# Attention with paged keys: products with new values on 32 rows, in pairs in the banks of the scores, added to the outputs by VectorE

## The chip, the cores and the metric

The kernel runs on one core of one Trainium2 chip. The metric is the device time of one execution in microseconds (us). Durations of single instructions come from one profiled execution.

## The reference

Two blocks with residuals over x (64 sequences, 32 positions, 512 channels). Block 0 is a state-space convolution over the positions and a feed-forward layer with low-rank experts. Block 1 is attention with a paged cache of keys and values, and another such feed-forward layer. The change lies in block 1's attention:

```
q, k, v = x Wq, x Wk, x Wv          # 32 query heads, 8 key heads, head size 128
q, k = rope(rmsnorm(q)), rope(rmsnorm(k))
k_all = [cache pages of the sequence (512 keys), its own 32 new keys]
v_all = [cache pages of the sequence (512 values), its own 32 new values]
probs = softmax(q k_all / sqrt(128), cached keys beyond the length masked out)
o = probs v_all                      # 4 query heads share one key head
out = o Wo
```

## The kernel before

The program has a prologue, block 0's feed-forward layer, the projection of queries, keys and values, attention, the output projection and block 1's feed-forward layer. A tensor `ps` covers PSUM: 8 banks of 128 partitions by 512 floats.

**Units, groups, batches.** `attention()` (from L1075) works through 512 units. A unit is one key head of one sequence (called a batch here): its four query heads times 32 positions make 128 rows of scores over 544 keys. Four units make a group (QU = 4), eight a batch (UB = 8), 16 one turn of the written-out loop (PER). There are 128 groups and 64 batches.

**Steps.** `turns` (L711) writes the loop of each engine as steps. In step u an engine does the stage "live(d)" for unit u - d; j is u within its turn plus the lead. So a unit passes through the engines over some ten steps:

- SP loads, per batch: the queries (L1122), 16 pages of keys (L1133, their numbers are read from the page table by L1129), the new keys (L1136), and the new values (L1141, `load_v`); then `store` sends the reciprocals of the sums (L1147) and the outputs `ot` of the batch (L1149). These are one queue in program order: for batch b it holds queries b+2, keys b+2, new values b+2, store b. The store waits for `s_o`, which ScalarE's copy of `ot` increments.
- VectorE splits the keys of two heads into an upper part in step u - 2 for even heads (`k_hi`, L1303) and a rest for odd heads (`k_lo`, L1306). PE's scores of an even head wait for the rest (`s_lo`). The first split of a batch, in steps 8b+2, waits for its keys. In steps 8b+2 and 8b+6 it also splits the queries' rest (`q_lo`, L1351), in steps 8b+3 it makes the mask (L1325).
- PE, u - 4: three products of the scores on split operands (L1227), into banks 0 and 1 for even units and 2 and 3 for odd ones; the 544 columns lie in the middle, columns 256 to 799 of each two banks. `wait(e, s_max, m - 1)` keeps it off banks that VectorE has not reduced.
- VectorE, u - 4: scales, masks, takes the row's extreme (L1319), to SBUF. ScalarE: exponential with row sums (L1392).
- PE, u - 6: four transposes of the probabilities of cached keys (L1236). ScalarE copies them to SBUF (L1379). Once a group, in step u - 7, one transpose takes the group's probabilities of new keys, 4 x 32 columns, to 128 rows (L1247), and ScalarE copies them to `pt_new` (L1384).
- PE, u - 8: products of the cached values with the transposed probabilities (L1260), summed in bank 5 or 6, one bank a group, 128 columns a unit.
- PE, u - 9, once a group: four products with new values (L1267). `v_new` holds the 32 new values of head k in rows 32k to 32k+31 and zeros elsewhere, so that a whole 128-row product gives head k's part only, and it goes onto the same sums:

```
for k in range(QU):
    last = e.matmul(sums(w, k), v_new[q][:, g // QU, k * D:(k + 1) * D], pt_new[:, w, :],
                    start=False, stop=(k == QU - 1), skip_group_check=True)
last.then_inc(s_nw, 1)
```

- ScalarE, u - 10, once a group: copies the bank to `ot` (L1374), increments `s_o`.
- POOL gathers the cached values of batch b+2 (L1182) once PE's new products of batch b are done (`s_nw`).

A float32 product is two records of PE in the trace, each with its weight load; a float32 transpose is one.

The last turn's steps are written out. There VectorE also does work for the output projection: L1333, L1339 and, in step PER+6, the split L1343 of the first outputs. The projection's first product (L1552) waits for `s_max`, its second unit for ScalarE's last copy.

In the prologue, L398 multiplies operands of 64 rows (upper and lower half in turn, 32 columns), between whole-array transposes of L386.

Of the kernel before, what the change touches and what calls it, by code (L numbers as in the profile page):

```python
# [19 lines left out]
ALU = mybir.AluOpType  # L20
# [3 lines left out]
P = 128  # L24
B, S, L = 64, 32, 512
# [12 lines left out]
KC = LK // P  # L38
# [658 lines left out]
def wait(eng, sem, value):  # L697

    if not isinstance(value, int) or value > 0:
        eng.wait_ge(sem, value)  # L700
# [374 lines left out]
def attention(nc, block, sems, ps, dram, cst, k_t, qk_t, v_own, o_t, ri_d, keys, results, early, projected, late):  # L1075
# [12 lines left out]
    with ExitStack() as ctx:  # L1088
# [12 lines left out]
        pt_new = sb("pt_new", [P, 2, P])  # L1101
        rt = sb("rt", [UB, 2, P])
        s_rows = sem("rows")
        s_v, s_one, s_idx, s_mask, s_qlo, s_hi, s_lo, s_s, s_max, s_e, s_ri, s_nc, s_c, s_cn, s_pt, s_wn, s_rt, s_nw, s_o = (
            sem(n) for n in ("v", "one", "idx", "mask", "qlo", "hi", "lo", "s", "max", "e", "ri", "nc", "c", "cn",
                             "pt", "wn", "rt", "nw", "o"))
        s_passed = [sem("passed_pool"), sem("passed_vector")]
        s_vr, s_vn = ([sem(f"{n}{q}") for q in range(2)] for n in ("vr", "vn"))
# [4 lines left out]
        turned = lambda w: ps[:, 6 - w, 0:2 * P]  # L1113
        sums = lambda w, k: ps[:, 5 + w, k * P:(k + 1) * P]

        steps = lambda e, step: turns(e, B * UB, PER, 12, step)

        @block.sync
        def _(e):
# [24 lines left out]
            def store(b, q):  # L1144
                e.wait_ge(s_rt, b + 1)
                at = bass.ds(b, 1) if not isinstance(b, int) else slice(b, b + 1)
                e.dma_start(ri_d[:, at, :].rearrange("g o x -> g (o x)"), rt[:, q, :]).then_inc(s_ot[q], 16)  # L1147
                e.wait_ge(s_o, (b + 1) * 2 + 1)
                e.dma_start(o_t[at, :, :].rearrange("o d x -> (o d) x"), ot[:, q, :]).then_inc(s_ot[q], 16)  # L1149

            e.wait_ge(s_in, 32)
            e.wait_ge(*own_stored)
            for q in range(2):
                e.wait_ge(s_one, q + 1)
                load_v(q, q)
            with e.Fori(0, B // 2 - 1) as i:
                for q in range(2):
# [20 lines left out]
        @block.gpsimd  # L1178
        def _(e):
            def gather_values(q):  # L1180
                for c in range(KC):
                    e.indirect_dma_start(out=v_raw[:, q, c, :], out_offset=None, in_=dram["v_cache"],  # L1182
                                         in_offset=bass.IndirectOffsetOnAxis(ap=idx[:, q, c:c + 1], axis=0)).then_inc(s_vr[q], 16)

            def indices(b, q):

                cols = slice(b * KC, (b + 1) * KC) if isinstance(b, int) else bass.ds(b * KC, KC)
                e.tensor_copy(idx[:, q, :], rows[:, cols]).then_inc(s_idx, 1)  # L1188

            e.wait_ge(s_qr, NQU * NT)  # L1190
            e.wait_ge(s_rows, 1)
            for q in range(2):
                indices(q, q)
                e.wait_ge(s_idx, q + 1)
                gather_values(q)
            e.wait_ge(s_proj, tiles - NT)
            e.memset(v_new[0][:, :, :], 0.0).then_inc(s_one, 1)
            e.wait_ge(s_proj, tiles)
            e.memset(v_new[1][:, :, :], 0.0).then_inc(s_one, 1)
            with e.Fori(0, B // 2 - 1) as i:  # L1200
                for q in range(2):
                    b = i * 2 + q
                    wait_apart(e, s_passed[0], (s_nw, (b + 1) * 2))
                    indices(b + 2, q)
                    wait_apart(e, s_passed[0], (s_idx, b + 3))
                    gather_values(q)

        @block.tensor
        def _(e):
            ident = cst[:, C_ID:C_ID + P]  # L1210

            def step(i, j, u, live):
                if live(4):
                    m, jj = u - 4, j - 4
                    g, q, r, w = jj % UB, (jj // UB) % 2, jj % 2, (jj // 2) % 2
                    if isinstance(u, int) and u < 6:
                        e.wait_ge(s_stage, tiles - 2 + 2 * (u - 4))
                    if g % QU == 0:
                        e.wait_ge(s_qlo, i * 4 + jj // QU + 1)
                    if g % 2 == 0:  # L1220
                        e.wait_ge(s_lo, i * UB + jj // 2 + 1)
                    wait(e, s_max, m - 1)
                    mine = slice(g * P, (g + 1) * P)
                    upper, lower = q_hi[:, q, mine], q_lo[q][:, mine]
                    for a, b, first, end in ((upper, k_hi, True, False), (upper, k_lo, False, False), (lower, k_hi, False, True)):
                        for part in (slice(0, W), slice(W, NKEY)):
                            last = e.matmul(scores(r)[:, part], a, b[:, w, g % 2, part],  # L1227
                                            start=first, stop=end)
                    last.then_inc(s_s, 1)
# [18 lines left out]
                if live(8):  # L1248
# [9 lines left out]
                    e.wait_ge(s_pt, m + 1)  # L1258
                    for c in range(KC):
                        e.matmul(sums(w, k), v_raw[:, q, c, g * D:(g + 1) * D], pt[:, jj % 4, c * P:(c + 1) * P],  # L1260
                                 start=(k == 0 and c == 0), stop=False, skip_group_check=True)
                if live(9) and (j - 9) % QU == QU - 1:
                    jj = j - 9
                    g, q, w = jj % UB, (jj // UB) % 2, (jj // QU) % 2
                    e.wait_ge(s_wn, i * 4 + jj // QU + 1)
                    for k in range(QU):
                        last = e.matmul(sums(w, k), v_new[q][:, g // QU, k * D:(k + 1) * D], pt_new[:, w, :],  # L1267
                                        start=False, stop=(k == QU - 1), skip_group_check=True)
                    last.then_inc(s_nw, 1)

            steps(e, step)

        @block.vector
        def _(e):
# [9 lines left out]
            v(lambda e: e.tensor_copy(lenf[:, :], leni[:, :]))  # L1284
            e.memset(mask[:, :, LK:NKEY], 0.0)
            e.wait_ge(s_qt, NQU * NT)

            def step(i, j, u, live):
                if live(6) and (j - 6) % QU == QU - 1:
# [20 lines left out]
                    split(j - 2)  # L1310
                if isinstance(u, int) and u == 4:
                    split(3)
                if live(4):
                    m, jj = u - 4, j - 4
                    q, r, k, w = (jj // UB) % 2, jj % 2, jj % QU, (jj // QU) % 2
                    at = slice(w * QU + k, w * QU + k + 1)

                    wait_apart(e, s_passed[1], (s_mask, i * 2 + jj // UB + 1), (s_s, m + 1), (s_e, m - 1))
                    e.tensor_tensor_reduce(out=sm[:, r, :], in0=scores(r), in1=mask[:, q, :],  # L1319
                                           scale=-SC, scalar=3e38, op0=ALU.add, op1=ALU.min,  # L1320
                                           accum_out=nm[:, at]).then_inc(s_max, 1)
# [40 lines left out]
        def _(e):  # L1362
# [47 lines left out]
                    e.activation(q_hi[:, q, :], qk[:, q, :], ACT.Copy).then_inc(s_qhi, 1)  # L1410

            steps(e, step)
        return s_max, s_nw, s_o


def by_head(x):
# [11 lines left out]
def output_projection(nc, block, sems, ps, dram, o_t, ri_d, results, late, attended):  # L1428
# [7 lines left out]
    PER = 2 * CB  # L1436
    sem = lambda n: sems.enter_context(nc.semaphore("op_" + n))
    w_raw, o_raw, ri_b, s_w, s_o, s_on, s_ot = results
    s_max, s_nw, s_copied = attended
    att, inputs = late.att, late.inputs  # L1440
    w_hi, w_lo, o_hi, o_lo = late.w_hi, late.w_lo, late.o_hi, late.o_lo
    s_whi, s_wlo, s_ohi, s_olo = late.s_whi, late.s_wlo, late.s_ohi, late.s_olo
# [31 lines left out]
    def _(e):  # L1474
# [6 lines left out]
                e.tensor_tensor(w_lo[par][:, r, :], w_raw[:, r, :], w_hi[par][:, r, :].bitcast(F32),  # L1481
                                ALU.subtract).then_inc(s_wlo, 1)
        e.wait_ge(s_nw, 2 * B)
        e.wait_ge(s_copied, 2 * B + 1)
        inputs.clear(e)
        halve(1, 1)
        with e.Fori(1, HK // 2) as i:
# [48 lines left out]
    def _(e):  # L1536
        def step(i, j, u, live):
# [4 lines left out]
                e.wait_ge(s_wlo, (i * 2 + j // CB + 1) * REP)  # L1542
            if isinstance(u, int) and u == 0:
                e.wait_ge(s_max, B * HK)
            if isinstance(u, int) and u == 1:
                e.wait_ge(s_copied, 2 * B + 1)
            e.wait_ge(s_ohi, u + 1)
            wait(e, s_acc, (u - 1) * KB)
            for ob in range(KB):
# [123 lines left out]
```

## Time and profile before

| | |
|---|---|
| Median of 3 runs | 2424.05 us (2423.72 to 2424.26) |
| Profiled execution | 2424.02 us, its span 2421.9 us |
| PE busy (matmuls) | 2374.0 us, 98% of the span |
| PE's weight loads | 2159.3 us, 89% |
| VectorE (DVE) | 1873.6 us, 77% |
| ScalarE (ACT) | 1320.2 us, 55% |
| GpSimd (POOL) | 720.4 us, 30% |
| Moved by DMA | 542.35 MB, 224 GB/s |

Busy time of PE counts the pipelined end of each matmul, so it says that PE never paused, not that it was used fully. The distance of starts in the timeline is what an instruction costs a stream. "x4" counts merged instructions, "[0.68 <-PE ...]" is the idle time of the engine before the row and what ended it. PEld is the weight load of PE, SPq the DMA queue of SP. Attention lies between some 790 and 1993 us.

### The profile page before, as it was taken

What the parts mean: (1) busy time and instruction counts of PE and PEld (TensorE: products, weight loads), DVE (VectorE), ACT (ScalarE), POOL (GpSimd) and SP (SyncE); (2) the same over time, 40 slices, a digit from 0 to 9 for tenths busy, and PEclk for the clock granted to TensorE, in tenths of its full rate; (3) what the DMA queues carried; (4) which work ended last, traced back from release to release, by engine and by line L of the source; (5) the groups of instructions that cost most, each with busy time, mean ns of one, the idle gap of its engine ahead of it and who ended that gap; (6) DMA issues with size and microseconds to landing.
All of it is one profiled execution on the core that took longest, in us unless ns stands there. A gap on an engine that the chain in (4) does not pass through costs nothing. (4 is left out here: it accounts for less than half of the span.)

```text
span 2421.9 us, 53973 instructions
## 1 busy us (share of the span) xinstructions
PE 2374.0 (98%) x16104; PEld 2159.3 (89%) x16104; DVE 1873.6 (77%) x3303; ACT 1320.2 (55%) x3759; POOL 720.4 (30%) x713
## 2 busy tenths in 40 slices
PE   5999999999999999999999999999999999999999
PEld 4888787887778999999999999999999998888877
DVE  6559999999961787888888888888888876666653
ACT  3335555555543777777777777777777771111120
POOL 2006666666641122222222222222222213131100
PEclk8999999999999999999999999999999999999999
DMA  9633333333337787888888888888888879665622
GB/s 340 237 122 92 95 95 95 97 116 95 96 119 238 241 302 278 294 302 297 289 285 297 301 294 282 292 300 304 285 285 298 301 268 295 217 224 198 219 70 104
DMA packets 434116, 542.35 MB, mean 224 GB/s; under 512 B 36980, under 2 KB 350100, under 8 KB 429460
## 3 DMA queue, kind: packets, MB, share of 16 engines
q1 hardware_dynamic: 391300, 398.43, 48.2%
q0 software_dynamic: 36864, 134.23, 16.4%
q10 hardware_dynamic: 5904, 9.06, 1.1%
q8 instruction: 28, 0.46, 0.1%
q14 instruction: 20, 0.16, 0.0%
HBM read 440.59 MB, written 101.01 MB: 224 GB/s over the span
## 5 line engine op out<-in xcount | busy, mean ns | idle before, releaser
L1319 DVE CUSTOM_DVE_ANT_0 at_sm<-ps,at_mask 128x544 f32<-128x544 f32 x512 | 370.1, 723 | 232.0 <-PE ps L1227 225.5
L1260 PE MATMUL ps<-at_pt,at_v_raw 128*128 128x128 f32 x4096 | 540.8, 275 | 0.0
L1260 PEld LDWEIGHTS ps<-at_pt,at_v_raw 128*128 128x128 f32 x4096 | 497.6, 192 | 0.0
L1379 ACT ACTIVATE at_pt<-ps 128x512 f32<-128x512 f32 x512 | 305.9, 598 | 292.2 <-PE ps L1236 279.7
L954 POOL TENSOR_TENSOR pr_m<-pr_qn,tb 128x256 f32<-128x256 f32 x320 | 331.3, 1054 | 311.4 <-DVE pr_qn L923 296.2
L1392 ACT ACTIVATE at_pr<-at_sm,at_nm 128x544 f32<-128x544 f32 x512 | 383.7, 750 | 15.6 <-DVE at_nm L1319 11.5
L1306 DVE TENSOR_TENSOR at_k_lo<-shared,at_k_hi 128x1088 fp32r<-128x1088 f32 x256 | 325.9, 1273 | 0.0
L772 PE MATMUL ps<-pr_hi,xh 128*128 (+1 forms) x768 | 317.5, 413 | 5.9 <-DVE pr_qn L923 4.8
L1182 POOL DMA_INDIRECT at_v_raw<-v_cache,at_idx x256 | 277.8, 1085 | 113.5 <-issue 62.1
L1236 PE MATMUL ps<-constants,at_pr 128*128 128x128 f32 x2048 | 306.9, 272 | 0.1
L774 PE MATMUL ps<-pr_hi,xl 128*128 (+1 forms) x768 | 303.2, 395 | 0.0
L773 PE MATMUL ps<-pr_lo,xh 128*128 (+1 forms) x768 | 303.0, 394 | 0.0
L880 ACT ACTIVATE pr_sq<-ps 128x128 f32<-128x128 f32 x640 | 168.6, 278 | 227.6 <-DVE f_a L916 222.2
L1188 POOL COPY at_idx<-at_rows 128x4 uint32 (+1 forms) x64 | 12.0, 188 | 852.3 <-PE ps L1267 786.2
L1227 PE MATMUL ps<-at_k_hi,at_q_hi 128*128 128x256 f32 (+1 forms) x1024 | 254.1, 329 | 0.6 <-issue 0.6
L1236 PEld LDWEIGHTS ps<-constants,at_pr 128*128 128x128 f32 x2048 | 243.1, 141 | 0.3 <-ACT at_pr L1392 0.3
L1227 PE MATMUL ps<-at_k_hi,at_q_lo 128*128 128x256 f32 (+1 forms) x1024 | 212.1, 289 | 0.0
L1227 PE MATMUL ps<-at_k_lo,at_q_hi 128*128 128x256 f32 (+1 forms) x1024 | 211.1, 287 | 0.0
L1500 ACT ACTIVATE op_ohi<-o_raw 128x2048 fp32r<-128x2048 f32 x31 | 59.5, 1920 | 268.2 <-PE ps L1557 223.7
L1552 PE MATMUL ps<-op_ohi,op_whi 128*128 128x512 f32 x512 | 199.3, 389 | 0.0
L1553 PE MATMUL ps<-op_ohi,op_wlo 128*128 128x512 f32 x512 | 199.2, 389 | 0.0
L934 DVE TENSOR_TENSOR pr_m<-pr_qn,ta 128x512 f32<-128x512 f32 x160 | 195.8, 1224 | 0.0
(233 smaller groups left out, 4283.6 us busy)
## 6 DMA issues: line engine op xcount, KB each, us to landing
shared<-k_t SPq DMA_DIRECT2D x1024, 128.0 KB, 4.1
qk_t<-pr_stage SPq DMA_DIRECT2D x160, 256.0 KB, 2.2
shared<-qk_t SPq DMA_DIRECT2D x64, 512.0 KB, 7.9
o_t<-at_ot SPq DMA_DIRECT2D x64, 512.0 KB
shared<-ri_d SPq DMA_DIRECT2D x32, 1024.0 KB, 8.3
o_raw<-o_t SPq DMA_DIRECT2D x32, 1024.0 KB, 6.0
f_w<-wqkv SPq DMA_DIRECT2D x12, 1024.0 KB, 6.1
s_k_in<-k_cache SPq DMA_DIRECT2D x16, 512.0 KB, 7.7
```

Of the source, the lines that this page charges most:

```text
L772: e.matmul(out, xh[:, k, cols], hi, start=(k == 0), stop=False)
L773: e.matmul(out, xh[:, k, cols], lo, start=False, stop=False)
L774: last = e.matmul(out, xl[:, k, cols], hi, start=False, stop=(k == KB - 1))
L954: ins = e.tensor_tensor(heads(m2[:, q, :])[:, :, a], heads(qn[:, q, :])[:, :, b], table(tb, i, j - 3, a), ALU.mult)
L1182: e.indirect_dma_start(out=v_raw[:, q, c, :], out_offset=None, in_=dram["v_cache"], in_offset=bass.IndirectOffsetOnAxis(ap=idx[:, q, c:c + ...
L1227: last = e.matmul(scores(r)[:, part], a, b[:, w, g % 2, part], start=first, stop=end)
L1236: last = e.transpose(ps_w(jj % 2)[:, c * P:(c + 1) * P], pr[:, w, k, c * P:(c + 1) * P], ident)
L1260: e.matmul(sums(w, k), v_raw[:, q, c, g * D:(g + 1) * D], pt[:, jj % 4, c * P:(c + 1) * P], start=(k == 0 and c == 0), stop=False, skip_gr ...
L1306: e.tensor_tensor(two(k_lo), raw, two(k_hi).bitcast(F32), ALU.subtract).then_inc(s_lo, 1)
L1319: e.tensor_tensor_reduce(out=sm[:, r, :], in0=scores(r), in1=mask[:, q, :], scale=-SC, scalar=3e38, op0=ALU.add, op1=ALU.min, accum_out=nm ...
L1379: e.activation(pt[:, jj % 4, :], ps_w(jj % 2), ACT.Copy).then_inc(s_pt, 1)
L1392: e.activation(pr[:, w, k, :], sm[:, r, :], ACT.Exp, bias=nm[:, at], scale=-1.0, accum_out=su[:, at]).then_inc(s_e, 1)
```

## The change

Each product with new values takes only rows 32k to 32k+31 of its operands. Its result no longer joins the sums: it goes to `fresh(k)`, 128 columns that the scores leave free in bank k (the first 128 for even k, the last 128 for odd k). Products 0 and 1 come as a pair at the head of PE's step u - 9, products 2 and 3 at the head of step u - 10, each ahead of the scores that go into the same two banks. PE's wait for `s_max` is moved to the head of the step. VectorE adds each pair to `ot` in SBUF, in steps u - 11 and u - 12, between its wait for the scores and its reduction. The store and the output projection wait for these additions (`s_added`), the projection with its first product. ScalarE's copy now takes the sums of cached values alone. The number of steps of lead is 13 in place of 12. The semaphore of the zeros is renamed.

```diff
+        fresh = lambda k: ps[:, k, k % 2 * (512 - P):k % 2 * (512 - P) + P]
+
+        def two_fresh(r):
+            x = ps[:, 2 * r, :]
+            return bass.AP(tensor=x.tensor, offset=x.offset, ap=[list(x.ap[0]), [2 * 512 - P, 2], [1, P]])
+
+        steps = lambda e, step: turns(e, B * UB, PER, 13, step)
...
-                e.wait_ge(s_o, (b + 1) * 2 + 1)
+                e.wait_ge(s_added, (b + 1) * 2)
                 e.dma_start(o_t[at, :, :].rearrange("o d x -> (o d) x"), ot[:, q, :]).then_inc(s_ot[q], 16)
...
+            def new_values(i, u, jj, r):
+
+                g, q, w, n = jj % UB, (jj // UB) % 2, (jj // QU) % 2, i * 4 + jj // QU
+                if isinstance(u, int) and u - 4 >= B * UB:
+                    e.wait_ge(s_max, B * UB)
+                    e.wait_ge(s_added, n)
+                e.wait_ge(s_wn, n + 1)
+                for k in range(2 * r, 2 * r + 2):
+                    own = slice(k * S, (k + 1) * S)
+                    last = e.matmul(fresh(k), v_new[q][own, g // QU, k * D:(k + 1) * D], pt_new[own, w, :], start=True, stop=True)
+                if r == 1:
+                    last.then_inc(s_nw, 1)
+
             def step(i, j, u, live):
+                if live(4):
+                    wait(e, s_max, u - 4 - 1)
+                for r in range(2):
+                    if live(9 + r) and (j - 9 - r) % QU == QU - 1:
+                        new_values(i, u, j - 9 - r, r)
...
-                    wait(e, s_max, m - 1)
...
-                                 start=(k == 0 and c == 0), stop=False, skip_group_check=True)
-                if live(9) and (j - 9) % QU == QU - 1:
...
+                                 start=(k == 0 and c == 0), stop=(k == QU - 1 and c == KC - 1), skip_group_check=True)
...
+            def add_new(i, j, live):
+
+                for r in range(2):
+                    if live(11 + r) and (j - 11 - r) % QU == QU - 1:
+                        jj = j - 11 - r
+                        q, at = (jj // UB) % 2, ((jj // QU) % 2 * QU + 2 * r) * P
+                        e.wait_ge(s_o, i * 4 + jj // QU + 2)
+                        mine = ot[:, q, at:at + 2 * P].rearrange("p (k x) -> p k x", k=2)
+                        ins = e.tensor_tensor(mine, mine, two_fresh(r), ALU.add)
+                        if r == 1:
+                            ins.then_inc(s_added, 1)
...
+                if not live(4):
+                    add_new(i, j, live)
                 if live(4):
...
                     wait_apart(e, s_passed[1], (s_mask, i * 2 + jj // UB + 1), (s_s, m + 1), (s_e, m - 1))
+                    add_new(i, j, live)
                     e.tensor_tensor_reduce(out=sm[:, r, :], in0=scores(r), in1=mask[:, q, :],
...
             if isinstance(u, int) and u == 0:
                 e.wait_ge(s_max, B * HK)
-            if isinstance(u, int) and u == 1:
-                e.wait_ge(s_copied, 2 * B + 1)
+                e.wait_ge(s_added, 2 * B)
```

## Rows read from the trace of the kernel before

**Rows 1.** Busy time by stages: us, PE, PEld, DVE, ACT, POOL, clock, DMA share, GB/s.
```profile
30.00:31.00 1.00, 1.00 (x46) 1.00 (x42) 0.73 (x4) 0.00 (x0) 0.00 (x0) 0.50 1.13 426
1300.00:1500.00 200.00, 200.00 (x1738) 199.78 (x1737) 162.63 (x334) 144.20 (x321) 51.11 (x55) 1.00 0.84 292
```
**Rows 2.** Timeline of ScalarE, the queries' split of two batches.
```profile
1490.70 1.04 ACT L1410 ACTIVATE at_q_hi<-shared 128x1024 fp32r<-128x1024 f32 x1
...
1509.48 1.04 ACT L1410 ACTIVATE at_q_hi<-shared 128x1024 fp32r<-128x1024 f32 x1
```
**Rows 3.** Groups of instructions by line, PE, whole span.
```profile
L1267 PE MATMUL ps<-at_pt_new,at_v_new 128*128 128x128 f32 x1024 | 135.4, 275 | 0.4 <-ACT at_pt_new L1384 0.4
```
**Rows 4.** Timeline of the weight loads, new products and the next scores.
```profile
1508.81 0.97 PEld L1267 LDWEIGHTS ps<-at_pt_new,at_v_new 128*128 128x128 f32 x8
...
1509.70 0.30 PEld L1227 LDWEIGHTS ps<-at_k_hi,at_q_hi 128*128 128x128 f32 x2
```
**Rows 5.** Timeline of PE and weight loads, prologue, L398 and the transposes behind.
```profile
29.84 0.30 PE L398 MATMUL ps<-s_er,s_ur 64*16 64x32 f32 x4
29.95 0.30 PE L398 MATMUL ps<-s_ei,s_ui 64*16 64x32 f32 x4
...
31.92 0.20 PE L398 MATMUL ps<-s_ei,s_ui 64*16 64x32 f32 x2
...
32.04 0.53 PEld L386 LDWEIGHTS ps<-constants,s_k_in 128*128 128x128 f32 x5
...
32.21 0.38 PE L386 MATMUL ps<-constants,s_k_in 128*128 128x128 f32 x2
```
**Rows 6.** Lines L287 and L1531: duration min/median/max in ns.
```profile
L287 DVE TENSOR_TENSOR s_ur<-s_small,s_er x1: 424/424/424, 25.8 to 25.8; 128x256 f32<-128x256 f32 x1
...
L1531 DVE TENSOR_TENSOR att<-att,ps x112: 673/681/689, 2047.5 to 2342.9; 128x512 f32<-128x512 f32 x112
```
**Rows 7.** Timeline of VectorE, first two steps of a batch's splits; last row the next batch.
```profile
1511.59 0.75 DVE L1303 CAST at_k_hi<-shared 128x1088 fp32r<-128x1088 f32 x1
1513.03 0.73 DVE L1319 CUSTOM_DVE_ANT_0 at_sm<-ps,at_mask 128x544 f32<-128x544 f32 x1 [0.68 <-PE ps L1227]
...
1514.28 1.28 DVE L1306 TENSOR_TENSOR at_k_lo<-shared,at_k_hi 128x1088 fp32r<-128x1088 f32 x1
1515.48 0.72 DVE L1319 CUSTOM_DVE_ANT_0 at_sm<-ps,at_mask 128x544 f32<-128x544 f32 x1
...
1530.37 0.76 DVE L1303 CAST at_k_hi<-shared 128x1088 fp32r<-128x1088 f32 x1
```
**Rows 8.** Timeline of SP's DMA queue: stores and last key transfers of two batches.
```profile
1495.09 0.37 SPq L1149 DMA_DIRECT2D o_t<-at_ot  x1
...
1507.30 0.33 SPq L1136 DMA_DIRECT2D shared<-qk_t  x1
...
1513.96 0.37 SPq L1149 DMA_DIRECT2D o_t<-at_ot  x1
...
1527.35 0.33 SPq L1136 DMA_DIRECT2D shared<-qk_t  x1
```
**Rows 9.** DMA issues, 900 to 1900 us: KB each, median us to landing.
```profile
shared<-qk_t SPq DMA_DIRECT2D x53, 512.0 KB, 7.9
shared<-qk_t SPq DMA_DIRECT2D x53, 128.0 KB, 2.9
```
**Rows 10.** DMA issues of the page, the same columns.
```profile
qk_t<-pr_stage SPq DMA_DIRECT2D x160, 256.0 KB, 2.2
```
**Rows 11.** Line L1303: what ended VectorE's idle time before it, us, times.
```profile
DMA shared<-qk_t: 1.7, 4
```
**Rows 12.** Timeline, the end of attention.
```profile
1991.58 2.29 DVE L1343 TENSOR_TENSOR op_olo<-o_raw,op_ohi 128x2048 fp32r<-128x2048 f32 x1 [1.10 <-ACT op_ohi L1403]
...
1992.65 0.19 PEld L1552 LDWEIGHTS ps<-op_ohi,op_whi 128*128 128x128 f32 x1
...
1992.96 0.60 ACT L1374 ACTIVATE at_ot<-ps 128x512 f32<-128x512 f32 x1 [1.12 <-PE ps L1267]
```

More of the change, by code:

```diff
@@ L1103, in attention @@
         s_rows = sem("rows")
-        s_v, s_one, s_idx, s_mask, s_qlo, s_hi, s_lo, s_s, s_max, s_e, s_ri, s_nc, s_c, s_cn, s_pt, s_wn, s_rt, s_nw, s_o = (
-            sem(n) for n in ("v", "one", "idx", "mask", "qlo", "hi", "lo", "s", "max", "e", "ri", "nc", "c", "cn",
+        s_v, s_added, s_idx, s_mask, s_qlo, s_hi, s_lo, s_s, s_max, s_e, s_ri, s_nc, s_c, s_cn, s_pt, s_wn, s_rt, s_nw, s_o = (
+            sem(n) for n in ("v", "added", "idx", "mask", "qlo", "hi", "lo", "s", "max", "e", "ri", "nc", "c", "cn",
                              "pt", "wn", "rt", "nw", "o"))
@@ L1114, in attention @@
         sums = lambda w, k: ps[:, 5 + w, k * P:(k + 1) * P]
-        steps = lambda e, step: turns(e, B * UB, PER, 12, step)
+        fresh = lambda k: ps[:, k, k % 2 * (512 - P):k % 2 * (512 - P) + P]
[3 more added lines that the diff above has]
+        steps = lambda e, step: turns(e, B * UB, PER, 13, step)
         @block.sync
@@ L1153, in _ @@
             for q in range(2):
-                e.wait_ge(s_one, q + 1)
+                e.wait_ge(s_rows, q + 2)
                 load_v(q, q)
@@ L1196, in _ @@
             e.wait_ge(s_proj, tiles - NT)
-            e.memset(v_new[0][:, :, :], 0.0).then_inc(s_one, 1)
+            e.memset(v_new[0][:, :, :], 0.0).then_inc(s_rows, 1)
             e.wait_ge(s_proj, tiles)
-            e.memset(v_new[1][:, :, :], 0.0).then_inc(s_one, 1)
+            e.memset(v_new[1][:, :, :], 0.0).then_inc(s_rows, 1)
             with e.Fori(0, B // 2 - 1) as i:
@@ L1260, in step @@
                         e.matmul(sums(w, k), v_raw[:, q, c, g * D:(g + 1) * D], pt[:, jj % 4, c * P:(c + 1) * P],
-                                 start=(k == 0 and c == 0), stop=False, skip_group_check=True)
-                if live(9) and (j - 9) % QU == QU - 1:
[L1263 to L1269, printed above, removed]
+                                 start=(k == 0 and c == 0), stop=(k == QU - 1 and c == KC - 1), skip_group_check=True)
             steps(e, step)
@@ L1412, in _ @@
             steps(e, step)
-        return s_max, s_nw, s_o
+        return s_max, s_nw, s_added
 def by_head(x):
@@ L1438, in output_projection @@
     w_raw, o_raw, ri_b, s_w, s_o, s_on, s_ot = results
-    s_max, s_nw, s_copied = attended
+    s_max, s_nw, s_added = attended
     att, inputs = late.att, late.inputs
@@ L1544, in step @@
                 e.wait_ge(s_max, B * HK)
-            if isinstance(u, int) and u == 1:
-                e.wait_ge(s_copied, 2 * B + 1)
+                e.wait_ge(s_added, 2 * B)
             e.wait_ge(s_ohi, u + 1)
```

## The prediction

> **What bounds the kernel now.** The page comes first: its line of busy tenths shows PE full from end to end, its parts 3 and 5 show heavy traffic and a busy VectorE. The table by stages places this in attention [rows 1]: in 200 us PE is busy for all 200.00, its weight loads for 199.78, VectorE for 162.63, ScalarE for 144.20; the granted clock is 1.00, the 2.4 GHz level, and the DMA engines are 84% taken. So attention runs at PE's pace, with two things near it: VectorE at 81% and the DMA engines. Attention is 128 groups of four units, two groups to a batch; the timeline of ScalarE, which splits the queries once a batch, gives the batch 18.78 us [rows 2].
>
> The products with new values are 1024 records of 275 ns as modelled [rows 3], but a record overlaps the next. What one costs PE is the distance of starts: the first load of a group's eight records is at 1508.81, the first load of the next scores at 1509.70 [rows 4]. That is 0.89 us for eight, 0.111 each, so 128 groups take 114 us of PE.
>
> **Removed and put back on PE.** A group's four products (two records each) become two pairs, each product on 32 rows. Streaming is by columns, 128 as before, so a pair can gain only by its two products running side by side: 4 x 0.111 = 0.446 becomes 2 x 0.111 = 0.223. The trace of before has one place with such products, the prologue's L398 (halves of 64 rows in turn). Four records of 32 columns take 0.11 us, starts at 29.84 and 29.95 [rows 5], with a granted clock of 0.50, the 1.2 GHz level [rows 1]. A 128-column record takes 0.111 at 2.4 GHz; a quarter of the columns at half the clock makes 0.055 each and 0.22 for four, so two do run side by side. The last two L398 records both start at 31.92 [rows 5], none is left over alone: the overlap is complete inside a pair too. TensorE: Matmul & The Clock Gate in the Trainium skill (The mechanism) has matmuls start strictly in program order; by that a pair would take three slots, 0.334 us, and PE's sum would rise by 28 us, which the ring below would still hide. By that rule the last two would not start together; the trace does not agree.
>
> What a pair pays is the change between split and whole array, in and out, as a pair stands alone between whole products. The same place shows one way out: the last split records start at 31.92 and stream 0.05 us, to 31.98; the first whole product's load is only at 32.04, and since its successor starts at 32.21 and streaming takes 0.11, its own stream begins at 32.10 [rows 5]. A gap of 0.13 us, where whole products follow each other with none [rows 4]. TensorEngine Tiling (Array Packing) in the Trainium skill (Key Properties) says that changing the mode drains the engine. By that rule every pair pays; the trace agrees, with its 0.13.
>
> The way in is not shown at a busy moment. I take 0.13 again. Lower bound of a change 0; upper bound: the next load waits until a record's modelled end, 0.164 after its successor could start, plus 0.06 from load to stream [rows 3 to 5], 0.22. So a pair costs 0.223 + 0.26 = 0.48 against 0.446: +0.04 x 256 pairs = **+9 us on PE** (between -57 with no gap and +57 at the upper bound; the two loads one behind the other would be another 0.06 x 256 = 15). The batch would take 18.93 us by PE alone.
>
> **VectorE's additions.** Two per group, 128x256, 256 in all. Nearest rows: 424 ns for 128x256 in SBUF, 681 for 128x512 with one operand in PSUM [rows 6]. I take 0.42: it is the same width, and 681 for twice the width gives no sign that PSUM costs more. Ends 0.35 (starts lie about 0.07 closer together than the durations say) [rows 7] and 0.68. That is 0.84 us in a group of 9.39, of which VectorE uses 7.6 [rows 1, 2]. It still fits, at 90%. They stand ahead of the unit's reduction, but the next scores into those banks, and the unit's transposes, come two steps of 2.1 to 2.3 us later, and before one reduction VectorE now idles 0.68 [rows 7]; that covers them. Cover gone, all would be exposed: 107 us. PE's wait for the reductions is the one it had, only ahead of the pairs. ScalarE's copy of the old sums moves with it by some 0.5 us, and its readers are steps away.
>
> **The moved wait on SP's queue.** This decides. Count steps by unit, eight to a batch: the store of batch b went out when ScalarE had copied (step 8b+17), the new one waits for the second addition, in step 8b+19. In before's time the reduction of that step starts at 1515.48 [rows 7]; with the first addition ahead of it by 0.36 and its own 0.42 the result is there at 1516.3, and with one more pair on PE at about 1516.8, against a store at 1513.96 [rows 8]. **SP stops some 2.8 us longer, and behind the store in its queue stand the queries and the 17 key transfers for batch b+3.** The queries, sent right behind the store of 1495.09 and 7.9 us under way [rows 8, 9], are split at 1509.48 [rows 2]: 6 us to spare. The keys have none: the last is issued at 1527.35 [rows 8], lands 2.9 us on [rows 9], at 1530.25, and VectorE splits it from 1530.37 [rows 7]; in four batches it already waits for them [rows 11].
>
> The wait closes a ring that before did not have. Keys of batch b+3 landed -> VectorE's split at step 8b+26 -> second addition of batch b+1, at step 8b+27 -> SP's store -> keys of batch b+4. One turn is one batch. Its length:
>
> - VectorE, by distances of starts [rows 7]: k_hi 1.44 less its idle 0.68 = 0.76 at most, taken 0.68 as the others lie 0.07 closer than they last; addition 0.36; reduction and q_lo 1.25; k_lo 1.20; addition 0.42 in full = 3.91.
> - Two hand-overs, landing to VectorE and VectorE to SP, an estimate of 0.12 each from the 0.12 between 1530.25 and 1530.37 = 0.24.
> - SP from the store to the last key transfer: 12.21 and 13.39 in two turns [rows 8], I take 12.9.
> - Landing: 2.9 among others' traffic, 2.2 for another kind elsewhere [rows 9, 10]; the gathers now run before the keys rather than with them: 2.45.
>
> Sum **19.5 us** (18.6 with 12.21 and 2.2; 20.5 with 13.39 and 2.9). Over PE's 18.93, so the ring sets the pace, and PE's +9 us hide in it. It turns for batches 3 to 63, 60 times: 60 x 0.72 = **+43 us**. The gathers wait for PE's product, not the addition, and are not delayed.
>
> **The end of attention.** PE's last pairs wait for the addition of the group before, which stands on VectorE behind the 2.29 us L1343 of the same unrolled steps, from 1991.58 to 1993.87; the projection's first product (1992.65) now waits for the last addition. Chain: 1993.87 + 0.42, pairs about 0.8, ScalarE's copy 0.60 with 0.1 of latency, two additions 0.8, 0.2 for semaphores = 1996.8 [rows 6, 12]. **+4 us**, exposed, as nothing else is ready for PE; 2 at least (had L1343 been early), 6 at most.
>
> **Sum.** Profiled execution 2424.02 (span 2421.9, 2.1 around it), the median of the runs is 2424.05, the same. 2424 + 43 + 4 + about 1 of PE in the first batches = **2472 us**.
>
> **Rivals.**
> *A, the ring (forecast), 0.55:* 2472; its own range 2450 to 2520.
> *B, PE sets the pace, 0.2:* keys land sooner than they did, the ring stays under 18.93. For it: the DMA engines are 84% taken on average [rows 1], and the keys move to a time with fewer gathers. Against: most of the turn is SP issuing one transfer after another. 2424 + 9 + 4 = 2437, up to 2485 with changes at 0.22.
> *C, faster, 0.13:* the changes cost nothing, or half of 0.13, and the ring is at its low end. PE alone would give 2424 - 57 + 4 = 2371, but the ring's 18.6 caps it: 60 x -0.18 = -11, so 2417. It decides from a ring under 18.7 and a change under 0.09.
> *D, VectorE short, 0.12:* at 90% it starts late from late keys, the next k_lo is late for PE within the same batch: additions at 0.68 put 0.52 on the ring, and half of the 0.68 of idle time that covers VectorE now [rows 7] is gone too: 2472 + 60 x 0.86 = 2524.
> That the pairs are not split at all is excluded by the operands, 32 rows of each.
>
> **Numbers.** Range 2432 to 2524: B's centre, A and most of D. What a measurement of this kernel can tell from no change is about 0.2%, 5 us. Faster 0.12 (most of C), same 0.06 (rest of C, edge of B), slower 0.82.
>
> **What would show it.** The period of a batch in the timeline, 19.5; VectorE idle before the first split of each batch, put down to the key transfer, in nearly all batches and about 1 us each; PE idle once a batch before the scores that need k_lo, 0.5 us; the store's issue some 7 us after the last new product; four records of a pair in two starts 0.11 apart, and the next whole load 0.1 or more behind; PE idle near the end of attention for 4 us. Wrong if the period is under 18.8, if VectorE doesn't wait for keys, or if PE is busy without gaps at a period above 19: then the changes of mode are dearer than I take them.

## The result and the profile after

| | before | after |
|---|---|---|
| Median (lowest to highest, 4 runs each) | 2424.09 us (2423.72 to 2424.26) | 2472.36 us (2471.99 to 2473.26) |
| Ratio to before | | 1.0194 [1.0182, 1.0206] |
| Profiled execution, its span | 2424.02, 2421.9 | 2472.7, 2470.9 |

The change makes the kernel 48 us slower; 2472 was predicted. The number held. Its largest step did not, as the rows and the runs below show.

The busy times of the page, the group of the new products, and those of the added and the waiting instructions on VectorE:

```profile
PE 2420.0 (98%) x16104; PEld 2143.3 (87%) x16104; DVE 1954.1 (79%) x3559; ACT 1323.9 (54%) x3759; POOL 756.2 (31%) x713
...
L1330 DVE CAST at_k_hi<-shared 128x1088 fp32r<-128x1088 f32 x256 | 194.5, 760 | 49.2 <-DMA shared<-qk_t 49.2
```

```profile
L1228 PE MATMUL ps<-at_pt_new,at_v_new 32*128 32x128 f32 x1024 | 125.1, 321 | 2.8 <-DVE at_ot L1311 2.8
L1311 DVE TENSOR_TENSOR at_ot<-at_ot,ps 128x256 f32<-128x256 f32 x256 | 106.1, 415 | 54.6 <-PE ps L1251 50.6 <-issue 2.0 <-ACT at_ot L1404 1.4
```

The sum of busy time of the new products hardly fell (125.1 us against 135.4 in [rows 3]), and says little of their cost, as records overlap. An addition lasts 0.415 us; 0.42 was taken. The same stretch as [rows 1], in the table by stages (us, then PE, PE's weight loads, VectorE, ScalarE, GpSimd, the granted clock, DMA share, GB/s):

```profile
1300.00:1500.00 200.00, 199.90 (x1676) 189.69 (x1676) 167.89 (x359) 139.69 (x310) 51.91 (x53) 1.00 0.85 280
```

PE is still full, its weight loads are not any more: 189.69 of 200 us where they had 199.78. PE counts as occupied, and yet for 10 us of the 200 no weight load is under way. VectorE rose to 84%, not to the 90% expected. In part that is the longer batch: in the run below with whole products and the old batch length it is 87% (174.72 of 200 us). The remaining 3 points are instructions that overlap: the busy time there grew by 0.57 us a group, where two additions last 0.83.

Where the 49.0 us between the spans lie, by the first weight load of four places in both timelines (before: 788.32, 1983.47, 1992.65, 2008.88; after: 787.91, 2026.79, 2040.02, 2057.88). The first two of before, then the four of after:

```profile
788.32 0.42 PEld L1227 LDWEIGHTS ps<-at_k_hi,at_q_hi 128*128 128x128 f32 x2
...
1983.47 0.30 PEld L1227 LDWEIGHTS ps<-at_k_hi,at_q_hi 128*128 128x128 f32 x2
```

```profile
787.91 0.43 PEld L1251 LDWEIGHTS ps<-at_k_hi,at_q_hi 128*128 128x128 f32 x2
...
2026.79 0.30 PEld L1251 LDWEIGHTS ps<-at_k_hi,at_q_hi 128*128 128x128 f32 x2
...
2040.02 0.19 PEld L1581 LDWEIGHTS ps<-op_ohi,op_whi 128*128 128x128 f32 x1 [1.84 <-issue]
...
2057.88 0.19 PEld L1581 LDWEIGHTS ps<-op_ohi,op_whi 128*128 128x128 f32 x1
```

| stretch | before | after | difference |
|---|---|---|---|
| up to attention's first scores | 788.32 | 787.91 | -0.4 |
| first to last scores | 1195.15 | 1238.88 | +43.7 |
| last scores to the projection's first product | 9.18 | 13.23 | +4.05 |
| the projection's first products (same work) | 16.23 | 17.86 | +1.6 |
| the rest | 413.0 | 413.0 | 0.0 |

The batches bring 43.7 us, the end of attention 5.7. A batch takes 19.47 us instead of 18.78: the queries' split on ScalarE comes at 990.48 and, 40 batches later, at 1769.43 (983.64 and 1734.84 before). What fills those 0.69 us is the question.

**Two signs that contradict each other.** The prediction's ring is the loop of keys, split, addition, store and next keys. VectorE does wait for the keys before the first split of a batch, as the ring asks for, and what ended its idle time is the key transfer, 60 times. This is its timeline:

```profile
1499.99 0.76 DVE L1330 CAST at_k_hi<-shared 128x1088 fp32r<-128x1088 f32 x1 [1.09 <-DMA shared<-qk_t]
1500.66 0.41 DVE L1311 TENSOR_TENSOR at_ot<-at_ot,ps 128x256 f32<-128x256 f32 x1
...
1502.23 1.28 DVE L1333 TENSOR_TENSOR at_k_lo<-shared,at_k_hi 128x1088 fp32r<-128x1088 f32 x1
1503.43 0.42 DVE L1311 TENSOR_TENSOR at_ot<-at_ot,ps 128x256 f32<-128x256 f32 x1
...
1519.45 0.76 DVE L1330 CAST at_k_hi<-shared 128x1088 fp32r<-128x1088 f32 x1 [1.09 <-DMA shared<-qk_t]
```

SP's store stands behind the second addition, where the prediction put it (1504.01 against an addition begun at 1503.43), and 7.5 us after the last new product of its batch, whose load is at 1496.51:

```profile
1484.89 0.36 SPq L1156 DMA_DIRECT2D o_t<-at_ot  x1
...
1497.35 0.33 SPq L1143 DMA_DIRECT2D shared<-qk_t  x1
...
1504.01 0.36 SPq L1156 DMA_DIRECT2D o_t<-at_ot  x1
```

But the list of waits shows almost nothing that PE would lose by it. PE stopped for the rest of the keys once, its weight loads four times:

```profile
PEld ps L1251 <- DVE at_k_lo L1333: 1.2, 4, 0.3
PE ps L1251 <- DVE at_k_lo L1333: 0.6, 1, 0.6
```

The rest of the keys is ready at 1503.51 (1502.23 + 1.28), and PE's load of the scores that read it comes only at 1503.90, behind a pair. PE is later than the keys, not the keys later than PE. The timeline of PE's weight loads shows what PE does instead:

```profile
1505.09 0.97 PEld L1284 LDWEIGHTS ps<-at_pt,at_v_raw 128*128 128x128 f32 x8
1506.18 0.30 PEld L1228 LDWEIGHTS ps<-at_pt_new,at_v_new 32*128 32x128 f32 x4
1506.60 0.30 PEld L1251 LDWEIGHTS ps<-at_k_hi,at_q_hi 128*128 128x128 f32 x2
```

The pair's four records start two by two; the second two, in a window of their own:

```profile
1506.29 0.19 PEld L1228 LDWEIGHTS ps<-at_pt_new,at_v_new 32*128 32x128 f32 x2
```

Eight whole loads 0.111 apart begin at 1505.09, 1505.20 and so on to 1505.87. The next would come at 1505.98; the pair's comes at 1506.18, **0.20 us later**. The pair is two starts, so it would be over at 1506.40; the next whole load is at 1506.60, again **0.20 us later**. A pair holds PE for 0.22 + 0.40 = 0.62 us, where two whole products took 0.446. Four pairs a batch: 4 x 0.174 = 0.70 us, which is the whole of the 0.69 us by which the batch grew.

### The profile page after: what moved, and what is told of

The parts are those of the page before. It is cut to its first block and busy times, and to the rows that moved or that the text cites. A ratio compares the mean times of both kernels' runs of the same rounds, so it can differ in the third digit from the quotient of the medians.

```text
span 2470.9 us, 54516 instructions
## 1 busy us (share of the span) xinstructions
PE 2420.0 (98%) x16104; PEld 2143.3 (87%) x16104; DVE 1954.1 (79%) x3559; ACT 1323.9 (54%) x3759; POOL 756.2 (31%) x713
## 5 line engine op out<-in xcount | busy, mean ns | idle before, releaser
L1189 POOL DMA_INDIRECT at_v_raw<-v_cache,at_idx x256 | 300.7, 1175 | 113.9 <-issue 62.4
L1195 POOL COPY at_idx<-at_rows 128x4 uint32 (+1 forms) x64 | 25.1, 392 | 860.9 <-PE ps L1228 794.4
L1330 DVE CAST at_k_hi<-shared 128x1088 fp32r<-128x1088 f32 x256 | 194.5, 760 | 49.2 <-DMA shared<-qk_t 49.2
```

## The experiments

A change of mode is the step from whole-array to 32-row products or back. The theory after this: the changes of mode, 0.20 us each, set the pace of the batches, and the ring of keys, addition and store is real but shorter than PE's stream. The rival is the prediction's own: the ring paces, and PE's gaps hide in it. The change has both causes. Of the next three kernels the first has only the ring, the second only the changes of mode, the third neither; the fourth is a control on the kernel before. All four ran beside the kernel before at 2425.02 us.

**Whole products in the new places, the store's wait as in the change.** The new products take all 128 rows again, but go to the same free columns, in the same steps; additions and waits stay.

```diff
-                for k in range(2 * r, 2 * r + 2):
-                    own = slice(k * S, (k + 1) * S)
-                    last = e.matmul(fresh(k), v_new[q][own, ...], pt_new[own, w, :], start=True, stop=True)
+                for k in range(2 * r, 2 * r + 2):
+                    last = e.matmul(fresh(k), v_new[q][:, ...], pt_new[:, w, :], start=True, stop=True)
```

> The changed kernel, but each product with new values takes all 128 rows again (zero-padded values), two at a time into the same free columns; additions and the store's wait stay. No change of the array's mode, so PE's own stream is the old one: 18.78 us a batch. Theory A (the ring keys, split, addition, store paces at 19.4 us or so): still 19.3 to 19.5 us a batch, PE now idles before scores that wait for k_lo, total 2424 + 60 x 0.6 + 6 = 2462 to 2475. Theory B (PE's stream of 19.46 us with split products is what paced; the ring only waits on itself): 2424 + 6 for the end of attention = 2430, batch 18.8 us.

Measured: 2457.32 us (2456.34 to 2457.68), ratio 1.0129 [1.0112, 1.0146]; a batch 19.22 us (985.78 and, 40 batches on, 1754.43 in ScalarE's timeline). Waits and the stretch of 1300 to 1500 us:

```profile
DVE at_k_hi L1329 <- DMA shared<-qk_t: 99.6, 61, 2.3
PEld ps L1250 <- DVE at_k_lo L1332: 21.8, 39, 1.0
PE ps L1250 <- DVE at_k_lo L1332: 15.0, 38, 0.8
```

```profile
1300.00:1500.00 200.00, 197.11 (x1696) 195.48 (x1695) 169.80 (x365) 139.33 (x314) 49.95 (x50) 1.00 0.88 287
```

Here the ring is what paces: PE stops for the rest of the keys 38 times, VectorE waits for the keys for twice as long as after the change, and PE is busy for 197.11 us of 200. Neither forecast held: B's 2430 is excluded, and A's 19.3 us and 2462 were a little high, so the ring is real, but shorter than the 19.47 us of the change.

**The store moved away, 32-row products kept.** The store of batch b-1 goes out behind the keys of batch b+2, when its addition has long been made; a transfer in SP's queue waits for nothing late any more.

```diff
                     load_keys(b + 2, q)
+                    if not (isinstance(b, int) and b == 0):
+                        store(b - 1, 1 - q)
                     e.wait_ge(s_nw, (b + 1) * 2)
                     load_v(b + 2, q)
-                    store(b, q)
```

> The changed kernel with SP's queue in another order: the store of batch b-1 goes behind the keys of batch b+2, so no key transfer stands behind a wait for an addition and the ring is open. Theory A (ring paces): VectorE's 49 us of waits for keys go, the time falls by what the ring was longer than PE's stream; PE's stream counted from pitches is 19.46 of 19.47 us, so even by A the gain is at most 1 to 15 us: 2457 to 2471. Theory B (PE's changes of mode pace): 2471 to 2473, batch 19.46 us, VectorE's waits gone.

Measured: 2474.02 us (2473.76 to 2474.11), ratio 1.0198 [1.0181, 1.0215], a batch 19.46 us. VectorE waits for no keys at all, and nothing is gained. The stretch is the change's own, PE full and its loads with 10 us of holes:

```profile
1300.00:1500.00 200.00, 200.00 (x1678) 189.88 (x1677) 168.55 (x360) 140.40 (x310) 51.82 (x53) 1.00 0.80 279
```

**Both: whole products and the moved store.**

> Both edits: whole-array products and the store behind the keys. Both theories: PE's stream alone, 18.78 us a batch, 2424 + 6 for the end of attention = 2430. With the run that only has whole products it gives the ring's price; with the run that only has the moved store it gives the price of the split, 60 to 64 batches x 0.69 = 42 to 44 us. If VectorE's additions cost anything by themselves it shows here, over 2430.

Measured: 2432.5 us (2428.61 to 2434.56, 10 runs), ratio 1.0029 [1.0019, 1.0039]; a batch 18.78 us, as before. The additions are all there and cost the batches nothing: from the first to the last scores it is 1195.31 us, before it was 1195.15. What is left against before, more than the 6 us expected, is the end of attention: 4.6 us more up to the projection's first product and 2.8 us more in its first products.

This run has the pair at the same place and with the same waits as the change, but with whole products:

```profile
1495.02 0.97 PEld L1289 LDWEIGHTS ps<-at_pt,at_v_raw 128*128 128x128 f32 x8
1495.91 0.53 PEld L1233 LDWEIGHTS ps<-at_pt_new,at_v_new 128*128 128x128 f32 x4
1496.36 0.30 PEld L1256 LDWEIGHTS ps<-at_k_hi,at_q_hi 128*128 128x128 f32 x2
```

```profile
1300.00:1500.00 200.00, 200.00 (x1739) 199.78 (x1738) 174.72 (x374) 144.64 (x321) 52.00 (x55) 1.00 0.83 290
```

The pair's load comes with no gap (1495.02 + 0.89 = 1495.91), the next scores' 0.45 us behind it, and over 200 us the loads have no holes. So it is not the place, the waits or the free columns that open the gaps, but the 32 rows.

**The moved store alone, in the kernel before.**

> The kernel before with only SP's order changed (store of batch b-1 behind the keys of batch b+2). A control for that edit: both theories say 2424, within 2 us, since PE never waited; the four waits for keys should go as the keys leave 1.2 us sooner.

Measured: 2424.73 us (2422.51 to 2426.64), ratio 0.9997 [0.9987, 1.0006]. The kernel before did not suffer from its store's place.

The change itself and the first three runs give the square:

| | store as in the change | store moved |
|---|---|---|
| whole products | 2457.3, batch 19.22 | 2432.5, batch 18.78 |
| 32-row products | 2472.4, batch 19.47 | 2474.0, batch 19.46 |

In the upper row, with whole products, the ring costs 25 us by itself (2457.3 - 2432.5; 60 batches x 0.44 = 26). In the right column the changes of mode cost 41.5 us by themselves (2474.0 - 2432.5), and 42.9 us from the first to the last scores in the traces (1238.16 - 1195.31). Together they don't add up, since both are paces of the same loop and the slower one counts: with 32-row products PE's stream is 19.46, and the ring of 19.22 disappears below it.

The trace of the change also shows the ring being held up by PE. From the first split of a batch to the store it is 4.02 us in most turns of both kernels with the store in the change's place (with whole products 1507.60 to 1511.62). After the change it is longer in others, up to 4.78 us. In this one VectorE stops for PE's scores ahead of the addition, and the store goes out 4.57 us after the split:

```profile
1206.64 0.92 DVE L1330 CAST at_k_hi<-shared 128x1088 fp32r<-128x1088 f32 x1 [0.18 <-DMA shared<-qk_t]
1207.86 0.42 DVE L1311 TENSOR_TENSOR at_ot<-at_ot,ps 128x256 f32<-128x256 f32 x1 [0.29 <-PE ps L1251]
```

**One pair of each group split, the other whole.** This asks for the price of a change of mode by another amount of it.

```diff
                for k in range(2 * r, 2 * r + 2):
-                    own = slice(k * S, (k + 1) * S)
+                    own = slice(k * S, (k + 1) * S) if r == 0 else slice(0, P)
```

> As the run with 32-row products and the moved store (2474.0), but only the first two products of each group take 32 rows; the other two take all 128 rows and still go to free columns. Against the run with whole products and the moved store (2432.5) one pair in each of 127 groups is changed. Theory (a change of mode costs TensorE 0.20 us each way, whatever the pair): one pair takes 0.22 + 0.40 = 0.62 us instead of 0.446, so +0.174 us x 127 = +22 us: 2454.6, half way to 2474.0, and the batch 19.13 us. Rival 1 (0.13 each way, as I had taken it before, and the rest of the time comes from something that both pairs together bring): 0.48 instead of 0.446, +5 us: 2437. Rival 2 (the addition's second read, not TensorE, sets the pace): no place half way, 2432 or 2474.

Measured: 2454.17 us (2452.33 to 2454.60), ratio 1.0118 [1.0101, 1.0135], a batch 19.11 us. That is half way, and +21.7 us for 127 pairs is 0.171 us a pair (the two medians come from different series; from the first to the last scores the traces have +21.9). Two changes are 0.171 + 0.223 = 0.39 us, 0.197 each. The 0.13 that the prediction took is excluded as the price of a change in this loop. The holes in the weight loads are half as large too:

```profile
1300.00:1500.00 200.00, 200.00 (x1709) 194.75 (x1707) 172.12 (x366) 141.31 (x315) 47.24 (x50) 1.00 0.83 292
```

**The last group done by whole products.** Of 128 groups only the last is added onto the sums by PE, ahead of ScalarE's copy, so that the projection waits for no late addition.

```diff
+                if is_last(n):
+                    if r == 0:
+                        for k in range(QU):
+                            last = e.matmul(sums(w, k), v_new[q][:, ...], pt_new[:, w, :], start=False, ...)
+                        last.then_inc(s_nw, 1)
+                    return
```

> The run with 32-row products and the moved store (2474.0) with one difference: the last group of the attention, alone of 128, is added onto the sums by TensorE with all 128 rows, before the one copy, so that no addition and only one step less stand between attention and output projection. Theory (the end of the attention costs 6 to 8 us: two idle stretches of TensorE of 2.8 and 1.8 us and then products at half the clock): 2466 to 2468, and the first products of the projection at full clock if the idle stretch stays under 2 us. Rival (the end costs what I predicted, 4 us, and the remaining 2 to 4 us are spread over the batches): 2470.

Measured: 2469.89 us (2468.79 to 2472.56), ratio 1.0186 [1.0169, 1.0203]. Against 2474.02 that is 4.1 us, which is the rival's number. The two medians come from different series, so they don't decide how large the end is. The traces place 5.0 us there: from the last product of the last scores to the end of the projection's first products it is 26.8 us with the last group whole, 31.8 in the run with the moved store. Of these, 2.1 us lie ahead of the projection's first product (11.14 against 13.22 us from the last scores; 9.18 before) and 2.9 in its first products (16.23 against 19.15; 16.23 before). So with the late additions the end costs 7.0 us there, as the theory has it. Part of it is the clock. After the change PE's weight loads stand idle for 2.97 and 1.84 us, and the projection's first products are 0.43 us apart; from 2044 us on they are 0.23 apart. The table by stages, of after:

```profile
2040.00:2044.00 4.00, 3.95 (x10) 3.16 (x11) 1.99 (x1) 1.91 (x1) 0.12 (x1) 0.57 0.35 133
2044.00:2047.00 3.00, 3.00 (x15) 2.44 (x13) 2.29 (x1) 0.00 (x0) 0.00 (x0) 1.00 0.24 31
```

and of the kernel with the last group whole, where they were idle for 0.47 and 1.69 us:

```profile
2036.00:2040.00 4.00, 3.63 (x16) 3.05 (x17) 2.32 (x2) 1.59 (x1) 0.20 (x1) 1.00 0.34 135
```

The granted clock is 0.57 in the one (for the most part the 1.2 GHz level) and 1.00 in the other. The limit of 2 us in the expectation is shown by no run.

**Four products at once.** If a change of mode is what costs, one change should serve all four products of a group. They are started one behind the other, each into a bank of its own: two in the scores' free columns as in the change, one directly onto its sum, one into the bank that the transposes have just left. ScalarE copies the last to SBUF (`fourth`), in step u - 9, and copies the sums there too, one step sooner than the change does; PE's next transposes wait for this. VectorE makes two additions, 128x256 and 128x128, in one step, u - 11. The store is moved and the last group is whole, as in the runs above.

```diff
-                for k in range(2 * r, 2 * r + 2):
+                wait(e, s_pt, u - 6)
+                for k, out in enumerate((fresh(0), fresh(1), sums(w, 2), ps_w(1)[:, 0:P])):
                     own = slice(k * S, (k + 1) * S)
-                    last = e.matmul(fresh(k), v_new[q][own, ...], pt_new[own, w, :], start=True, stop=True)
-                if r == 1:
-                    last.then_inc(s_nw, 1)
+                    last = e.matmul(out, v_new[q][own, ...], pt_new[own, w, :], start=(k != 2), stop=True, ...)
+                last.then_inc(s_nw, 1)
...
+                    e.activation(fourth[:, (jj // QU) % 2, :], ps_w(1)[:, 0:P], ACT.Copy)
                     e.activation(ot[:, q, t * QU * P:(t + 1) * QU * P], ps[:, 5 + t, :], ACT.Copy).then_inc(s_o, 1)
...
+                    e.tensor_tensor(own, own, fourth[:, w, :], ALU.add).then_inc(s_added, 1)
```

> All four 32-row products of a group are started one behind the other, on four row tiles, into four different banks (two in the scores' free columns, one directly onto its sum, one in a bank of the transposes, from which ScalarE copies it), once a group; the store is moved as before, and the last group is done with all rows. Theory (a change of mode costs 0.20 us each way and products on different row tiles go side by side): a group takes TensorE 0.22 + 0.40 = 0.62 us instead of 0.893 whole, 127 x 0.276 = 35 us less than the run with whole products and moved store less its end (2432.5 - 6 = 2426): 2391, a batch 18.25 us, faster than both kernels. Rival 1 (only two products go side by side, whatever the banks): 0.85 us a group, 2421. Rival 2 (another wait takes the pace once TensorE is shorter: keys, VectorE's additions or ScalarE's second copy): above 2400, and TensorE idle once a batch or a group at that place. Rival 3 (a change costs more when it stands ahead of a wait): above 2410 with the gaps of the change longer than 0.2 us.

Measured: **2391.00 us** (2388.16 to 2392.74), ratio to before **0.9857 [0.9840, 0.9873]**: faster than both kernels, by 35 us (before took 2425.67 beside it) and by 81 us. A batch takes 18.25 us. The timeline of PE's weight loads:

```profile
1504.09 0.97 PEld L1302 LDWEIGHTS ps<-at_pt,at_v_raw 128*128 128x128 f32 x8
1505.18 0.31 PEld L1245 LDWEIGHTS ps<-at_pt_new,at_v_new 32*128 32x128 f32 x8
1505.62 0.30 PEld L1267 LDWEIGHTS ps<-at_k_hi,at_q_hi 128*128 128x128 f32 x2
```

The last of the eight whole loads is at 1504.87, the next would be at 1504.98 and comes at 1505.18: 0.20 us for the way in. From there to the next whole load it is 0.44 us, where a pair took 0.42 (1506.18 to 1506.60 above). Four products go side by side in the time of two. The group costs PE 0.64 us instead of 0.89. The forecast of 2391 was met, and none of the three rivals. The stretch shows PE and VectorE closer to each other than in any other kernel here, VectorE at 89%:

```profile
1300.00:1500.00 200.00, 200.00 (x1789) 194.44 (x1788) 177.75 (x384) 149.22 (x351) 51.21 (x55) 1.00 0.87 302
```

**The same with the store in the change's place.**

> The run with four products at once, but with the store of a batch back in its old place, behind the same turn's loads of new values and ahead of the next keys. Theory (the ring of store, keys, split and addition is 19.2 us a batch when the last addition comes 12 steps behind, as measured with whole products, and takes one step less, 2.3 us, when it comes 11 steps behind: 16.9 us, below TensorE's 18.25): 2391 as with the store moved, and no batch in which TensorE waits for keys. Rival (the ring is not set by the addition's step but by the transfers, and stays near 19.2 us): 2391 + 60 x 0.95 = 2448, with VectorE waiting for keys in nearly all batches, as with whole products. Between them, a ring of 18.6 us would give 2412.

Measured: 2392.06 us (2391.25 to 2392.66), ratio 0.9864 [0.9847, 0.9880], a batch 18.25 us, and in the list of waits:

```profile
DVE at_k_hi L1343 <- DMA shared<-qk_t: 3.0, 2, 1.8
```

The same store in the same place of SP's queue costs nothing here. The addition it waits for comes one step sooner, and no reduction, no rest of the queries and no rest of the keys stand on VectorE between the split and the addition any more:

```profile
1510.74 0.80 DVE L1343 CAST at_k_hi<-shared 128x1088 fp32r<-128x1088 f32 x1
1512.22 0.42 DVE L1324 TENSOR_TENSOR at_ot<-at_ot,ps 128x256 f32<-128x256 f32 x1 [0.68 <-PE ps L1261]
...
1513.07 0.36 SPq L1161 DMA_DIRECT2D o_t<-at_ot  x1
```

From split to store it is 2.33 us instead of 4.02, and 0.68 of that is VectorE waiting for PE. So the ring is shorter by 4.02 - 1.65 = 2.37 us, by estimate 19.22 - 2.37 = 16.9 us, which fits the prediction's chain. That it lies below 18.25 is shown; the 16.9 is not, as no kernel ran at it.

## Why the prediction was right, and where it was not

**What bounds the kernel: right.** Attention runs at PE's pace, before and after.

**A pair runs side by side: right.** Two products of two records each are two starts 0.11 apart. TensorE: Matmul & The Clock Gate in the Trainium skill (The mechanism) has matmuls start strictly in program order; that would make three slots of a pair and five of four products, 0.33 and 0.56 us. The pair's 0.22 and the four's 0.24 (0.44 less the 0.20 of the way out) don't agree with that.

**The price of a change of mode: this term failed.** The prediction took "a gap of 0.13 us" from one place in the prologue and "0.13 again" for the way in, and so "+9 us on PE". It is 0.20 us, both ways, in the loop. PE's term is 254 x 0.174 = +44 us and not +9 (the pairs of the last group are in the end's account). The prediction's upper bound, 0.22, +57 us, held it. The one place it had was at the other level of the clock (0.50 granted), with 64-row products of 32 columns, and its stream's end was inferred, not seen; which of these makes the difference no run tells apart. TensorEngine Tiling (Array Packing) in the Trainium skill (Key Properties) says that changing the mode drains the engine. The traces agree in that the cost comes once for a stretch of split products, not once for each of them: 0.42 us from the first split load to the next whole one with two products inside, 0.44 with four.

**The additions: right.** 0.415 us each, and with whole products and the moved store they leave the batch at 18.78 us. The load on VectorE was put too high, 90% against 87% there.

**The ring: it exists and was sized closely, but it isn't what paces.** The prediction gave it 19.5 us, 18.6 to 20.5; alone it is 19.22 us. On the average of its turns the last key's issue to the split takes 2.39 us (2.45 and a hand-over of 0.12 were taken), the split to the store 4.05 (3.91 and 0.12), the store to the last key 12.78 (12.9). "Over PE's 18.93, so the ring sets the pace, and PE's +9 us hide in it" is the sentence that is wrong, and only because the 18.93 is wrong. PE's stream is 19.46 us, and the ring hides in PE. That 60 x 0.72 = +43 came out as measured (+43.7) is a coincidence: the ring as estimated, 19.5 us, is as long as PE's stream really is. By mechanism the case is rival B, "PE sets the pace", at the upper part of its span (2437, "up to 2485 with changes at 0.22"): 2424 + 44 + 5.7 = 2474. B's own condition, a ring under 18.93, did not hold either; the ring is longer than that, and only the dearer changes lift PE above it. The forecast had 0.55 on the ring and 0.2 on B, so its number is right by luck.

**What should have shown it.** The prediction named both signs. VectorE's wait for the keys was there in 60 batches and about 1 us long, and yet proves nothing: VectorE runs ahead of PE, and its waiting costs nothing as long as the rest of the keys is there before PE asks. PE idle once a batch for 0.5 us was missing, and "PE is busy without gaps at a period above 19: then the changes of mode are dearer than I take them" was what the profile showed.

**The end of attention: a little dearer.** +4.05 us to the projection's first product, as predicted (+4). The 1.6 us of the projection's first products at the lower clock were not foreseen; in the other runs whose last group is added late they are 2.4 to 2.9 us. The "about 1 us" of the first batches lies inside the stretch from the first to the last scores, where 43 + 1 was predicted and 43.7 measured. The 0.4 us that attention began earlier has nothing to do with it.

## What to carry to other kernels

Splitting the array for a small contraction is paid per change between split and whole, here 0.20 us each way at 2.4 GHz, which is nearly two whole 128-column records of this kernel (0.111 each). So gather all small products of a step behind one change: two at a time lost 0.17 us a pair, four at a time won 0.25 us a group (0.27 by the batches, 18.78 to 18.25 for two groups), with the same arithmetic.

When two loops could pace a kernel, remove each alone and both together before believing either. An engine that waits is a sign of the pace only if the engine that is full is made to wait for it in turn; look at who is later at the meeting point.

A wait put into a DMA queue ahead of the next loads ties its condition to them. Here it cost 25 us with the work waited for 12 steps behind, and nothing in a kernel that has it 11 steps behind, ahead of the other work of that step. So either move the transfer behind those loads or its condition ahead.

## What the hardware showed beyond that

- A change between 32-row and whole products costs PE 0.20 us going in and 0.20 us coming out (1505.98 to 1506.18, 1506.40 to 1506.60), the same for two products inside and for four (0.42 and 0.44 us from the first split load to the next whole one).
- Four f32 products of 32 rows and 128 columns, on four groups of rows and into four banks, take 0.24 us (0.44 less the 0.20 of the way out), four whole ones 0.89: a factor of 3.7. With the two changes the factor is 1.4 (0.89 to 0.64). TensorEngine Tiling (Array Packing) in the Trainium skill (Theoretical Speedup) has up to 4 for such a size. The traces agree inside a stretch of split products, not with its changes counted.
- PE's busy time doesn't show the gaps: it is 199.90 of 200 us with some 16 us of changes inside (41 pairs in 200 us, 0.40 each). The weight loads' busy time shows something of them, 189.69 against 199.78 [rows 1].
- After 2.97 and 1.84 us without a weight load, a last group's pairs between them, the granted clock was 0.57 over the next 4 us. After 3.08 and 1.84 us, with whole products and the store moved, it was 0.50 over the next 4.1 us. After 0.47 and 1.69 us it stayed at 1.00.
